# Decayed attention on one core: next values and gate products at a period's end, PSUM freed by copies, 64 clock matmuls, low parts shared in the last period

## The reference, cut to what matters

```python
xn = layernorm(x)
q, k = rope(l2norm(xn @ Wq)), rope(l2norm(xn @ Wk)); v = xn @ Wv
clock = softplus(xn @ clock_W + clock_b)               # one number per token
g = exp(clip(cumsum(-softplus(xn @ gate_W + gate_b)), -60, 50))
q = q * g;  k = k / (g + 1e-8)
p = xn @ p_W + p_b                                     # the logits
p_exp = exp(p - max_over_tokens(p)) * clock
q = q / (cumsum(p_exp) + 1e-8);  k = k * p_exp
out = softmax(causal(q @ k.T / sqrt(128))) @ v @ out_W + out_b + x
```

## Time and profile before

| | |
|---|---|
| Median of 3 runs | 2843.98 us (2842.98 to 2850.35) |
| Profiled execution | 2843.84 us, its span 2842.0 us |
| Mean granted TensorE clock | 0.958 of 2.4 GHz |
| Decayed attention | 2420.4 to 2670.3 us of the span, 249.9 us |
| Busy over the span | TensorE 93%, VectorE 78%, ScalarE 64%, POOL 43% |

### The profile page before, as it was taken

One profiled execution on the slowest core, in us unless ns is written; L12 is line 12 of the kernel. 1 busy time (PEld: TensorE's weight loads), 2 busy tenths in 40 slices (PEclk: granted clock), 3 DMA queues, 4 the chain that ended last, 5 costly groups with the idle time before them and its releaser, 6 DMA issues. The chain is left out here.

```text
span 2842.0 us, 36493 instructions
## 1 busy us (share of the span) xinstructions
PE 2640.8 (93%) x11651; PEld 1988.8 (70%) x11651; DVE 2230.7 (78%) x3334; ACT 1827.1 (64%) x3084; POOL 1234.3 (43%) x1271
## 2 busy tenths in 40 slices
PE   7899999997999999999999987999999988787788
PEld 4688888865666666666666655888888865666566
DVE  6787777777999999999999967877877755366445
ACT  3455555556888888888888853555555554265465
POOL 3466766663332323323232322667666621144300
PEclk9999999998999999999999999999999999588799
DMA  2566666634333333333333313666666500000000
GB/s 81 115 143 146 131 145 147 131 89 156 98 107 104 101 104 98 107 101 104 104 100 104 97 45 84 147 141 138 147 138 141 119 8 24 16 15 1 8 8 30
DMA packets 107391, 271.62 MB, mean 96 GB/s; under 512 B 30656, under 2 KB 35648, under 8 KB 107072
## 3 DMA queue, kind: packets, MB, share of 16 engines
q1 hardware_dynamic: 82192, 235.48, 33.5%
q0 software_dynamic: 24576, 33.62, 4.3%
q10 hardware_dynamic: 432, 0.20, 0.0%
HBM read 258.42 MB, written 10.76 MB: 95 GB/s over the span
## 5 line engine op out<-in xcount | busy, mean ns | idle before, releaser
L628 POOL TENSOR_TENSOR moe_experts_lo<-moe_experts_hidden,moe_experts_hi 128x512 fp32r<-128x512 f32 x512 | 662.6, 1294 | 340.6 <-ACT moe_experts_hi L566 340.6
L909 DVE TENSOR_TENSOR heads_e_lo<-heads_e,heads_e_hi 128x1024 fp32r<-128x1024 f32 x512 | 616.1, 1224 | 26.0
L573 ACT ACTIVATE psum<-psum 128x512 f32<-128x512 f32 x512 | 298.0, 582 | 478.5 <-PE psum L90 478.5
L743 POOL DMA_DIRECT2D heads_left<-heads_parts x512 | 307.4, 616 | 671.1 <-PE psum L797 611.5
L849 ACT ACTIVATE heads_e<-psum 128x1024 f32<-128x1024 f32 x512 | 520.7, 1024 | 106.5 <-PE psum L797 106.5
L600 DVE TENSOR_TENSOR moe_experts_weighted<-moe_spread,psum 128x512 f32<-128x512 f32 x512 | 351.1, 686 | 190.5 <-PE psum L90 186.6
L88 PE MATMUL psum<-heads_e_hi,heads_v_lo 128*128 128x512 f32 x1024 | 429.5, 419 | 18.1 <-DVE heads_u L875 18.1
L88 PE MATMUL psum<-moe_n_hi,moe_w_lo 128*128 128x512 f32 x1024 | 400.8, 391 | 5.8 <-PEq L54 5.8
L89 PE MATMUL psum<-heads_e_lo,heads_v_hi 128*128 128x512 f32 x1024 | 404.3, 395 | 0.0
L90 PE MATMUL psum<-heads_e_hi,heads_v_hi 128*128 128x512 f32 x1024 | 401.4, 392 | 0.0
L89 PE MATMUL psum<-moe_n_lo,moe_w_hi 128*128 128x512 f32 x1024 | 400.0, 391 | 0.0
(11 more groups left out here) (410 smaller groups left out, 4319.1 us busy)
## 6 DMA issues: line engine op xcount, KB each, us to landing
moe_spread<-moe_mask SPq DMA_DIRECT2D x128, 1024.0 KB, 10.1
heads_right<-heads_parts SPq DMA_DIRECT2D x512, 64.0 KB
heads_left<-heads_parts POOLq DMA_DIRECT2D x512, 64.0 KB, 2.4
heads_scale<-heads_inverse_copy SPq DMA_DIRECT2D x64, 512.0 KB, 3.7
moe_experts_raw<-in_gate SPq DMA_DIRECT2D x16, 256.0 KB, 11.8
moe_experts_raw<-in_up SPq DMA_DIRECT2D x16, 256.0 KB, 11.7
moe_experts_raw<-in_down SPq DMA_DIRECT2D x16, 256.0 KB, 11.7
heads_parts<-heads_e_hi SPq DMA_DIRECT2D x16, 256.0 KB, 2.4
```

The source lines that it names most:

```text
L573: act.activation(psum[:, GATE + p % 2, :], psum[:, GATE + p % 2, :], ACT.Silu).then_inc(silu_ready, 1)
L628: pool.tensor_tensor(lo[:, p, :], hidden[:, p % 2, :], f(hi[:, p, :]), ALU.subtract).then_inc(low_ready, 1)
L743: eng.dma_start(f(tile[row:row + 2 * HEAD, h % 2, :]), parts_dram[dims, order:order + 2, at]).then_inc(loaded[h % 2], 16)
L909: dve.tensor_tensor(e_lo[:, s, :], e[:, s % 4, :], f(e_hi[:, s, :]), ALU.subtract).then_inc(low, 1)
```

## The change

- TensorE computes the values of batch b, and the gate product of batch b + 1, in the last slot of the period that prepares batch b. The gate of batch 0 goes ahead of everything. The other steps of the preparation move up by one slot; the sum of the rotated parts and the product with the gain on POOL too. The logit product stands ahead of the clock matmuls.
- At the end of a half ScalarE copies SUMS (`take_sums`) and VectorE copies OUT (`take_values`) to SBUF. The next half waits for these two copies. `invert` and `leave` read the copies, one or two slots later.
- The two columns that move in the clock matmuls are now the high and the low part of the weights, so two matmuls for each tile of tokens, 64 in all. VectorE adds the two columns (`tick_sums`). The weight in DRAM is a column of 128 numbers, loaded last of the weights; it was 128 x 128.
- In the last period VectorE makes the low part of every second unit (`by_vector`), POOL the others.

The diff, cut to its core:

```diff
 e = sb(f"{tag}_e", [P, RING, BANK])
 e_hi, e_lo = (sb(f"{tag}_e_{part}", [P, RING, BANK], F32R) for part in ("hi", "lo"))
-inverse, check = (sb(f"{tag}_{name}", [P, HALVES, BANK]) for name in ("inverse", "check"))
+sums, raw, inverse, check = (sb(f"{tag}_{name}", [P, HALVES, BANK]) for name in ("sums", "raw", "inverse", "check"))
...
+
+def by_vector(n):
+
+    return n >= (BATCH - 1) * COUNT and n % 2 == 1
+
+def take_low(eng, who, n):
+    at = slice(first_of(n % COUNT), BANK)
+    eng.wait_ge(e_high, n + 1)
+    eng.tensor_tensor(e_lo[:, n % RING, at], e[:, n % RING, at], f(e_hi[:, n % RING, at]),
+                      ALU.subtract).then_inc(e_low[who], 1)
+
+def wait_low(eng, n):
+    if n >= 0:
+        who = "vector" if by_vector(n) else "pool"
+        eng.wait_ge(e_low[who], sum(by_vector(i) == by_vector(n) for i in range(n + 1)))
...
-                weights = [part[:, 0:2] for part in w["clock"]]
-                pe.matmul(out, n_lo[:, at], weights[0], start=j == 0, stop=False, skip_group_check=True)
-                pe.matmul(out, n_hi[:, at], weights[1], start=False, stop=False, skip_group_check=True)
-                last = pe.matmul(out, n_hi[:, at], weights[0], start=False, stop=j == TOKENS // P - 1,
+                pe.matmul(out, n_lo[:, at], w["clock"], start=j == 0, stop=False, skip_group_check=True)
+                last = pe.matmul(out, n_hi[:, at], w["clock"], start=False, stop=j == TOKENS // P - 1,
                                  skip_group_check=True)
             last.then_inc(products["clock"], 1)
...
+        def gate(b):
+            after(pe, side["k"]["sine"], b)
+            project(b, "gate", ONE)
+
         def prepare(b, slot):
             if slot == 1:
-                after(pe, side["k"]["sine"], b)
-                project(b, "gate", ONE)
+                after(pe, v_low, b)
+                project(b, "logit", OTHER)
                 if b == 0:
                     ticks_of_all()
-            elif slot == 2:
-                after(pe, v_low, b)
-                project(b, "logit", OTHER)
-            elif slot == 4:
-                pe.wait_ge(abs_ready, b + 1)
+            elif slot == 3:
                 pe.wait_ge(greatest_ready, b + 1)
                 project(b, "q", ONE)
-            elif slot == 5:
+            elif slot == 4:
                 pe.wait_ge(gain_exp, b + 1)
                 project(b, "q_swap", OTHER)
-            elif slot == 6:
...
-                pe.wait_ge(tick_abs, 1)
-                pe.wait_ge(tick_greatest, 1)
+                pe.wait_ge(tick_sums, 1)
...
             if s == 0:
-                after(pe, out_ready, a * HALVES + half)
-            pe.wait_ge(e_low, n + 1)
+                after(pe, sums_taken, a * HALVES + half)
+                after(pe, values_taken, a * HALVES + half)
+            wait_low(pe, n)
...
-            if a is not None and slot == 0:
-                pe.wait_ge(floor_ready, a + 1)
-                values(a)
             if b is not None:
                 prepare(b, slot)
             if a is not None and slot >= LATE:
                 weighted_values(a, slot - LATE)
-
+            if b is not None and slot == SLOTS - 1:
+                pe.wait_ge(floor_ready, b + 1)
+                values(b)
+                if b + 1 < BATCH:
+                    gate(b + 1)
+
+        gate(0)
...
-            z = psum[:, SCORES, 0:64].rearrange("p (j two) -> p j two", two=2)[:, :, 0]
-            act.wait_ge(products["clock"], 1)
-            act.activation(ticks[:, 0, :], z, ACT.Abs, bias=columns["clock_b"]).then_inc(tick_abs, 1)
+            act.wait_ge(tick_sums, 1)
+            act.activation(ticks[:, 0, :], ticks[:, 1, :], ACT.Abs, bias=columns["clock_b"]).then_inc(tick_abs, 1)
...
-            if slot == 2:
+            if slot == 0:
                 act.wait_ge(products["gate"], b + 1)
                 after(act, divisor, b)
                 act.activation(decay, pair(ONE), ACT.Abs, bias=columns["gate_b"]).then_inc(abs_ready, 1)
+            elif slot == 1:
                 act.wait_ge(abs_ready, b + 1)
                 act.activation(decay, decay, ACT.Exp, scale=-1.0).then_inc(exp_ready, 1)
-            elif slot == 3:
...
+        def take_sums(a, half):
+            n = a * HALVES + half
+            act.wait_ge(out_done, a * COUNT + ENDS[half] + 1)
+            after(act, checked, n - 1)
+            act.copy(sums[:, half, :], psum[:, SUMS, :]).then_inc(sums_taken, 1)
+
         def invert(a, half):
             n = a * HALVES + half
-            act.wait_ge(out_done, a * COUNT + ENDS[half] + 1)
+            act.wait_ge(sums_taken, n + 1)
             after(act, added, n - 1)
-            act.activation(inverse[:, half, :], psum[:, SUMS, :], ACT.Ln).then_inc(sums_log, 1)
+            act.activation(inverse[:, half, :], sums[:, half, :], ACT.Ln).then_inc(sums_log, 1)
...
+            if a is not None and slot == 0:
+                if a > 0:
+                    take_sums(a - 1, 1)
+                value_highs(a)
+            if a is not None and slot == ENDS[0] + LATE + 1:
+                take_sums(a, 0)
             if a is not None and slot < COUNT:
                 weights(a, slot)
-            if a is not None and slot == 0 and a > 0:
+            if a is not None and slot == 1 and a > 0:
                 invert(a - 1, 1)
-            if a is not None and slot == 1:
-                value_highs(a)
-            if a is not None and slot == ENDS[0] + LATE + 1:
+            if a is not None and slot == ENDS[0] + LATE + 2:
                 invert(a, 0)
...
+        take_sums(BATCH - 1, 1)
         invert(BATCH - 1, 1)
...
-            z = psum[:, SCORES, 0:64].rearrange("p (j two) -> p j two", two=2)[:, :, 0]
+            both = psum[:, SCORES, 0:64].rearrange("p (j two) -> p j two", two=2)
+            dve.wait_ge(products["clock"], 1)
+            dve.tensor_reduce(ticks[:, 1, :], both, mybir.AxisListType.X, ALU.add).then_inc(tick_sums, 1)
             dve.wait_ge(tick_abs, 1)
-            dve.tensor_scalar(ticks[:, 1, :], z, columns["clock_b"], 0.0, ALU.add, ALU.max).then_inc(tick_greatest, 1)
+            dve.tensor_scalar(ticks[:, 1, :], ticks[:, 1, :], columns["clock_b"], 0.0, ALU.add,
+                              ALU.max).then_inc(tick_greatest, 1)
...
+            elif slot == 9:
+                sine(b, "k", ONE)
             elif slot == 10:
-                sine(b, "k", ONE)
+                weigh(b, "q", total, queries_ready)
             elif slot == 11:
-                weigh(b, "q", total, queries_ready)
-            elif slot == 12:
                 weigh(b, "k", log, key_factor)
                 low(b, "q", q)
-            elif slot == 13:
+            elif slot == 12:
                 low(b, "k", k)
...
+        def take_values(a, half):
+            n = a * HALVES + half
+            dve.wait_ge(out_done, a * COUNT + ENDS[half] + 1)
+            after(dve, out_ready, n - 1)
+            dve.tensor_copy(raw[:, half, :], psum[:, OUT, :]).then_inc(values_taken, 1)
...
-            dve.tensor_tensor(check[:, half, :], inverse[:, half, :], psum[:, SUMS, :], ALU.mult).then_inc(checked, 1)
...
-            dve.scalar_tensor_tensor(out=inverse[:, half, :], in0=psum[:, OUT, :], scalar=-1.0,
+            dve.wait_ge(values_taken, n + 1)
+            dve.scalar_tensor_tensor(out=inverse[:, half, :], in0=raw[:, half, :], scalar=-1.0,
                                      in1=inverse[:, half, :], op0=ALU.mult, op1=ALU.mult).then_inc(out_ready, 1)
...
-            if a is not None and slot == 0 and a > 0:
-                leave(a - 1, 1)
-            if a is not None and slot == 1:
+            if a is not None and slot == 0:
+                if a > 0:
+                    take_values(a - 1, 1)
                 value_lows(a)
             if a is not None and slot == ENDS[0] + LATE + 1:
-                leave(a, 0)
+                take_values(a, 0)
             if b is not None:
                 prepare(b, slot)
+            if a is not None and slot == 2 and a > 0:
+                leave(a - 1, 1)
+            if a is not None and slot == ENDS[0] + LATE + 3:
+                leave(a, 0)
+            if a == BATCH - 1 and slot < COUNT and by_vector(a * COUNT + slot):
+                take_low(dve, "vector", a * COUNT + slot)

         periods(step)
+        take_values(BATCH - 1, 1)
...
-            if a is not None and slot < COUNT:
-                n, first = a * COUNT + slot, first_of(slot)
-                pool.wait_ge(e_high, n + 1)
-                pool.tensor_tensor(e_lo[:, n % RING, first:BANK], e[:, n % RING, first:BANK],
-                                   f(e_hi[:, n % RING, first:BANK]), ALU.subtract).then_inc(e_low, 1)
+            if a is not None and slot < COUNT and not by_vector(a * COUNT + slot):
+                take_low(pool, "pool", a * COUNT + slot)
+            if b is not None and slot == 6:
+                sum_rotated(b, "q")
             if b is not None and slot == 7:
```

(11 more changed lines are left out.)

47 lines of the change are left out of this document (25 added, 22 removed).

## The result

Changed: 2815.36 us, median of 4 runs (2813.48 to 2817.04). Before, in the same comparison: 2846.14 us (2842.98 to 2850.35). The ratio is 0.9893, with an interval of 0.9878 to 0.9909: faster by 31 us, where I had forecast 45, and 0.4 us outside my range, which is less than the spread of the four runs.

The account below looks back on a forecast made before the run. The stage was taken as bound by a chain hopping between engines, none full. Periods -7.5 - 11.0 - 9.0 - 11.2 - 12.5 = -51.2, plus 3.6 and 2.6 added back, gave -45: 2843.98 to 2799 us, range 2787 to 2815.

Parts of the forecast that it names:

- the last one of the sum: Whole program: 2843.98 us minus the stage's 45 gives 2799 us, with no correction due.
- Rival 1: Appended products and the scores after them: TensorE runs at 1.2 GHz, clock eats part of the gain; 2812 us, chance 0.12.
- Second and third period: Middle of the decayed attention: 51.8 to 40.8 us (-11.0) and 50.6 to 41.6 us (-9.0).
- the wait of the weighted values for the low part behind the sum of k: Middle periods, after the key squares: TensorE waits 1.9 us for the last low part, made by POOL.
- half of the difference: Products ending two periods: half the gap between 4.1 us (2.4 GHz) and 7.7 us (1.2 GHz), +3.6 us added back.
- VectorE and POOL, 2.6 us in all: Over the stage: VectorE operations blocked by POOL, two blocks of 1.3 us added back.
- rival 2: Middle periods: VectorE becomes the bound, waiting for POOL, 3 to 5 us more each; 2808 to 2814 us, chance 0.10.
- Fourth period: Middle period with no gate behind it: 51.5 to 40.3 us, -11.2.
- First period: Chain of clock matmuls: gate and logit first, 64 matmuls at 0.2117 us, transpose 7.5 us earlier; 55.4 to 47.9 us.
- rival 3: First period: clock matmuls start at 2.4 GHz, 3.2 us more go; with no blocking 2788 us, chance 0.05.
- Last period: End of stage: loses 24 values, the 4.8 us wait and pipeline waits, shares low parts; 40.6 to 28.1 us, -12.5.
- The mid-period wait: Before the second half's first value matmul: 3.40 us wait becomes two side-by-side copies, 0.6 and 0.7 us; under 1 us.

Follow-up runs that it names:

- e12: Changed kernel plus thrown-away wide matmuls keeping TensorE busy before both norms behind the stage, attention unaltered: 2797.45 us, 0.984 of before.
- e1: Changed kernel with the next batch's value products moved ahead of a period's last weighted values: 2796.45 us, 0.984 of before.
- e3: Changed kernel plus eight thrown-away 512-column matmuls before the last weighted values of a period: 2797.11 us, 0.983 of before.
- e6: Changed kernel without the copies of SUMS and OUT, inversion and outputs back in their old slots: 2835.35 us, 0.997 of before.
- e8: Order of e1, with VectorE instead of POOL doing the keys' product with the gain and the sum of k: 2791.30 us, 0.982 of before.
- e2: Changed kernel with POOL making a period's last low part before the sum of k, not after: 2805.44 us, 0.986 of before.
- e4: Changed kernel with values back behind a period's first scores and gate before the logit product: 2839.90 us, 0.998 of before.
- e7: Changed kernel with 96 clock matmuls (32 thrown away) and all low parts on POOL: 2818.42 us, 0.992 of before.
- e10: Changed kernel keeping the copies, but with inversion and outputs moved to the same early places as in e6: 2841.93 us, 0.999 of before.
- e11: The changed kernel run once more, nothing altered: 2811.43 us, one run.

## Why the prediction was wrong, point by point

- **The step that failed** is the last one of the sum. I took the stage's -45 from the time of the whole program, 2843.98 - 45, with everything outside the stage at nothing. The only reason given was that "the change touches only the decayed attention"; "so no correction is due" weighs the profiled execution against the median and says nothing of the rest. The rest of the program grew by 10.5 us: its two norms are granted 0.50 and 0.61 in their first 15 us, where they had 0.84 and 0.94. In e12, with TensorE busy ahead of both, they are at 1.00, the 10.5 us are gone, and 2.9 more, since the norms of the kernel before had a cold stretch too (0.84 and 0.94). So the clock is enough to account for them. Of the 16.4 us between 2799 and 2815.36, to a few tenths, 10.5 are this, 2.3 the stage, 2.5 its later start, and 1.3 lie between the profiled execution and the median. Rival 1 counted on a lower clock, but only inside the periods.
- **What stays open** is what makes the clock come back late in a norm. The length of the wait ahead of it does not tell: e1 and the changed kernel have the same 6.34 us of idle ahead of the first norm, the same 2.48 ahead of the second, and 171.4 against 182.2 us. In the runs without added matmuls there the two norms are either both mostly hot (0.81 and more: before, e1, e3, e6, e8) or both cold (0.50 and 0.61 to 0.64: changed, e2, e4, e7, e10, e11).
- **Luck in the stage.** That its sum came within 2.3 us hides larger errors. The three middle periods fell 12.8 us short of their -31.2; against that stood the 6.2 us that I had added back for the clock and for VectorE beside POOL, and 4.4 us that the first and the last period gave beyond their forecast.
- **Second and third period, -6.5 and -3.7 instead of -11.0 and -9.0.** I had named the wait of the weighted values for the low part behind the sum of k, and sized it 1.9 us; it was 2.6, and what I missed is its sequel: I gave the products "half of the difference" for the clock, and they paid most of it in both (7.1 and 6.7 us against 4.1). e3 prices that at 2.8 us per period, e1 the gap and the clock together at 4.3. The layout also had the matmuls behind the key squares at a granted clock of 1.00, as they had been. They are at 0.54 now; the windows before and after:
```profile
2566.98:2570.50 3.52, 3.52 (x20) 3.03 (x21) 2.66 (x3) 1.77 (x4) 1.11 (x2) 1.00 0.02 5
```
```profile
2540.66:2544.40 3.74, 3.74 (x13) 3.21 (x13) 3.71 (x4) 0.31 (x1) 2.21 (x1) 0.54 0.00 0
```
What that costs no run shows, since TensorE waits for POOL's low part behind it.
- **VectorE and POOL, 2.6 us in all**: too little. The two divisor operations and the product of q stood beside POOL's and took 3.08, 2.19 and 3.38 us in the third period, 3.9 us more than the durations of before that the layout had used:
```profile
2564.84 1.66 DVE L1406 SCALAR_TENSOR_TENSOR decay_attend_total<-decay_attend_total,decay_attend_decay 128x1024 f32<-128x1024 f32 x1
2566.53 1.91 DVE L1410 SCALAR_TENSOR_TENSOR decay_attend_total<-decay_attend_greatest,decay_attend_total 128x1024 f32<-128x1024 f32 x1
...
2570.68 1.23 DVE L1362 TENSOR_TENSOR decay_attend_q_rotated<-decay_attend_q_rotated,decay_attend_total 128x1024 f32<-128x1024 f32 x1 [1.03 <-ACT decay_attend_total L1280]
```
A duration read from the old order did not hold in the new one. In the rows of the changed kernel further up the cosine product (L1381), which reads PSUM, takes 1.22 us beside POOL's low part; the operation after it (L1437), with both inputs in SBUF, takes 3.08 us beside POOL's product, and 1.73 in e8 with POOL's low parts beside it. That the place of the inputs decides this, no run shows. The operations that cost most were not the ones that the copies gave a second input in SBUF (0.68 to 1.34 us, 0.69 without POOL); they had both there before. e8 gives back 1.4 to 2.7 us per period, so rival 2 was right in kind. Its part was smaller than the clock's in the second and third period, and the larger one in the fourth.
- **Fourth period, -8.2 instead of -11.2.** No gate behind it, no cold products (granted clock 0.95 over the period); the keys came late, at S+43.2 instead of S+40.3. Ahead of them stood the divisor operations, 3.12 and 2.19 us, and four output operations that took 5.9 us together (the residual alone 2.75) where the layout had 2.9. e8 takes 2.7 us of the 3.0 back.
- **First period, -10.5 instead of -7.5.** This is rival 3. Behind the gate and logit products the first clock matmuls are 0.11 us apart. While they run back to back the clock falls again (granted 0.95 from 2428.2 to 2432.0, 0.50 from there to 2438.8), so the 64 take 10.4 us, not 13.5:
```profile
2428.22 0.17 PE L1144 MATMUL psum<-decay_w_clock,decay_n_lo 128*128 128x2 f32 x1
...
2438.44 0.35 PE L1145 MATMUL psum<-decay_w_clock,decay_n_hi 128*128 128x2 f32 x1
```
- **Last period, -13.9 instead of -12.5**: right in sum, wrong in one of its terms. I counted on the shared low parts; e7 shows that they bring nothing. The copies (5.6 us by e10 against e6) and the values' absence from the front (7.9 us by e4) carry it.
- **The mid-period wait** went as forecast: from 3.40 to 0.22 us. But my account of *why* the copies pay was wrong: removing that wait alone brings nothing in the middle periods (e10 against e6), where another takes its place. They pay there because the outputs can be made later.
- **A reading that was off**: "half of the time at 1.2 GHz" in the third period. Its granted clock was 0.50 from 2527.6 to 2538.4, 0.75 from 2556 to 2562, 0.52 in the last 2.2 us and 0.98 or more over the rest: about a third of the time at 0.50, some 16 us, which fits the 0.84 of the whole. No term of the sum rests on it.

## What to carry over

Where the granted clock varies as it does here, a stage cannot be summed up alone: ask what the stretch behind it will be granted, and measure stage and rest apart (-42.7 and +10.5 us here). Work that is moved next to a short gap can pay the gap twice, as the products behind the 2.6 us of idle did, once as idle and once as clock (1.5 and 2.8 us here); put independent products into the gap, not behind it. And when a copy frees a buffer, look for what it allows to be reordered: in the third and fourth period two moves were each worth nothing or less alone, and 3.7 and 8.2 us together.

## What was not expected of the hardware

Throwing matmuls away made the program faster twice: 3 x 8 of them at the ends of periods (e3, 6.1 us of stage), and 38 ahead of the two norms (e12, 13.4 us of 182.2). And the same unchanged code ran for 171.4 us behind one version of the stage and for 182.2 us behind another, and for 182.2 us again when that program was run again. With TensorE busy, the clock came back about 3 us after a norm's first matmul in one kernel and about 15 us after it in another.
